# An attention and mixture layer on one Trainium2 core: the start and the end of the program are written in another order

## The reference, cut to what matters

```python
xn = _layernorm(x)
q = (einsum('bte,oe->bto', xn, Wq) + bq) * 16 ** -0.5
kv = einsum('bte,oe->bto', xn, Wkv) + bkv             # k, v: 16 channels each
qr = q.reshape(b, 16 * 512, 16)                       # 8192 query rows a batch
p = softmax(einsum('brd,bsd->brs', qr, k))
attn = heads_back(einsum('brs,bsd->brd', p, v)) @ Wo.T + bo
# mixture: e of 6 experts by xn @ w_gate (the largest), tokens = A @ B
a = softmax(xn @ tokens[e].T / 16)
delta = ((a[:, 1:] @ (tokens @ wt.T + wt_b)[1:] + xn) @ wd.T + wd_b) * scale
out = x + attn + xn + log(exp(delta) for the chosen expert)
```

## Time and profile before

| | |
|---|---|
| median of three runs | 924.08 us (920.78 to 924.17) |
| profiled execution | 922.81 us |
| its span, first to last instruction | 921.0 us |
| PE busy | 857.4 us, 93% of the span |
| DVE busy | 780.7 us, 85% |
| ACT busy | 673.2 us, 73% |
| POOL busy | 512.8 us, 56% |
| mean granted TensorE clock | 0.971 |
| chain of waits that ended last | PE 78%, DVE 15%, issue 3%, POOL 2% |

### The profile page before, as it was taken

The page is one execution under the profiler, slowest core; times in us unless marked ns, Lnnn a source line. Parts: engine busy times, 40 slices in busy tenths (PEclk is TensorE's granted clock), DMA queues, the critical chain, the costliest instruction groups (busy, mean ns, idle before and its releaser), DMA issues.

```text
span 921.0 us, 17722 instructions
## 1 busy us (share of the span) xinstructions
PE 857.4 (93%) x5845; PEld 282.1 (31%) x5845; DVE 780.7 (85%) x1490; ACT 673.2 (73%) x1369; POOL 512.8 (56%) x691
## 2 busy tenths in 40 slices
PE   4479999999999999999999999999999999999895
PEld 2223222332323333332323333332333333232222
DVE  6578898988989898998989898998989898899814
ACT  2115787787878778777877877787778778788880
POOL 2656566565666656565666647566666656534200
PEclk9676999999999999999999999999999999999998
DMA  3423243534524453543335353442444453331110
GB/s 96 97 66 60 74 92 92 117 83 116 113 75 105 107 114 94 124 87 108 95 94 111 94 116 87 129 100 86 96 113 104 104 115 84 92 94 61 48 60 34
DMA packets 125072, 86.04 MB, mean 93 GB/s; under 512 B 57143, under 2 KB 109112, under 8 KB 124984
## 3 DMA queue, kind: packets, MB, share of 16 engines
q1 hardware_dynamic: 124824, 84.82, 38.3%
q10 hardware_dynamic: 160, 0.10, 0.1%
HBM read 39.30 MB, written 33.54 MB: 79 GB/s over the span
## 4 chain that ended last, share of the span: by engine, by line
PE 78%; DVE 15%; issue 3%; POOL 2%; ACT 1%; DMA 1%; ACTq 0%; POOLq 0%; DVEq 0%
PE pO L364 24%; PE pA L346 18%; DVE M L808 9%; PE pB L351 8%; PE pA L481 5%; PE pA L428 5%; PE pA L499 4%; PE pA L483 3%; PE pA L417 3%; PE pA L453 2%; PE pA L468 2%; DVE st L728 2%; PE pB L461 1%; DVE RL L821 1%; PE pB L439 1%
## 5 line engine op out<-in xcount | busy, mean ns | idle before, releaser
L808 DVE TENSOR_REDUCE M<-pA 128x1 f32<-128x512 f32 x1024 | 652.3, 682 | 86.4 <-PE pA L346 82.3
L627 ACT ACTIVATE P<-pB 128x512 f32<-128x512 f32 x1002 | 552.6, 601 | 130.5 <-PE pB L351 126.0
L346 PE MATMUL pA<-K,Q 48*128 48x512 f16 x1024 | 326.0, 388 | 21.7 <-DVE M L808 11.8
L351 PE MATMUL pB<-Q,K 50*128 50x512 f16 x1002 | 317.8, 385 | 0.3 <-DVE M L808 0.3
L364 PE MATMUL pO<-P,VK 128*32 128x512 f32 x2048 | 273.7, 607 | 3.1 <-ACT OTr L633 2.0
L346 PEld LDWEIGHTS pA<-K,Q 48*128 48x128 f16 x1024 | 67.8, 94 | 343.6 <-DVE M L808 287.7
L954 POOL TENSOR_SCALAR Cz<-Cx 128x512 f32<-128x512 f32 x32 | 62.1, 1940 | 37.0 <-ACT Cx L609 37.0
L499 PE MATMUL pA<-wo,On 128*128 128x256 f32 x248 | 71.9, 414 | 2.7 <-DVE RL L821 2.7
L364 PEld LDWEIGHTS pO<-P,VK 128*32 128x32 f32 x2048 | 40.4, 108 | 99.3 <-issue 63.2
L351 PEld LDWEIGHTS pB<-Q,K 50*128 50x128 f16 x1002 | 64.3, 94 | 11.8 <-ACT P L627 10.3
L968 POOL TENSOR_TENSOR On<-Op,Rb 128x512 f32<-128x512 f32 x31 | 39.9, 1286 | 45.0 <-issue 41.2
(11 more groups left out here) (148 smaller groups left out, 806.6 us busy)
## 6 DMA issues: line engine op xcount, KB each, us to landing
o_parts<-OTr SPq DMA_DIRECT2D x62, 256.0 KB, 2.3
X<-in_x SPq DMA_DIRECT2D x16, 512.0 KB, 3.9
q_pieces<-Qp SPq DMA_DIRECT2D x64, 128.0 KB
out<-OUT SPq DMA_DIRECT2D x32, 256.0 KB, 3.9
Op<-o_parts SPq DMA_DIRECT2D x31, 256.0 KB
Rb<-l_parts SPq DMA_DIRECT2D x31, 256.0 KB
Q<-q_pieces SPq DMA_DIRECT2D x30, 256.0 KB, 4.8
Q<-q_pieces SPq DMA_DIRECT2D x34, 128.0 KB, 4.5
```

The source lines that it names most:

```text
L346: e.matmul(bank1("ab", t)[:, :], Q16[r:r + 48, b % 3, h, 128 * s:128 * s + 128], K16[r:r + 48, b % 3, :], start=True, stop=True).then_inc( ...
L351: e.matmul(bankB(t)[:, :], K16[r:r + 50, b % 3, 128 * i:128 * i + 128], Q16[r:r + 50, b % 3, :, 32 * hh:32 * hh + 32], start=True, stop=Tr ...
L627: e.activation(P[:, u % PR, :], bankB(u + LB)[:, :], ACT.Exp, scale=alpha).then_inc(S("e"))
L808: e.tensor_reduce(M[:, t // 32 % 2, t % 2, t % 32 // 2:t % 32 // 2 + 1], bank1("ab", t)[:, :], AX, ALU.max, negate=True).then_inc(S("mx"))
```

## The change

Batch 1 gets a table of its own, `SECOND`, and its x is loaded in the setup, ahead of the biases. Its statistics and normalisation come before batch 0's first tile. 56 and 12 products of a 128x128 identity with itself, written to `pO`, are put ahead of `rg` and behind `bs` (`warm0`, `warm1`). `uke` of batch 0 goes from VectorE to ScalarE, and `vge` of batch 0 before the K DMAs. Each of the two writes of Q to HBM waits only for its own piece. `bw0`, `bw1`, `w2` go from before the first tile to slots 6.4 to 12.4, and the first batch's `s` to `radd0` four slots later. At the end the second products of the last 44 tiles go in fours instead of twos, `o0` to `o3` of the last batch follow the last two `pv`, and `sl0` and `o3` take a bank of the second group and `sl1` one of the first.

```diff
+    "utm": -30, "s": 9, "smax": 9.6, "sexp": 10.2, "ssum": 10.8, "snorm": 11.4, "p": 17, "pte": 17.6, "a": 21, "mm": 21.6,
+SECOND = {
+    "stats0": -125.9, "stats1": -125.8, "stats2": -125.7, "stats3": -125.6, "aggr": -125.5, "var": -124, "root": -115.3,
+    "refine": -113.9, "norm": -113.8, "ph": -113.6, "pl": -107, "xtd": -102.5,
+}
...
-        put("ab", n - n % 2 + 0.02 * (n % 2), n)
+        put("ab", n - n % 2 + 0.02 * (n % 2) if n < NT else n - n % 4 + 0.02 * (n % 4), n)
...
-            "bd": lambda t: (S("e"), t - LB + 1), "sl0": lambda b: (S("rl"), 4),
+            "bd": lambda t: (S("e"), t - LB + 1), "sl1": lambda b: (S("rl"), 8),
...
-            "sl1": lambda b: (S("rl"), 8),
+            "sl0": lambda b: (S("rl"), 4),
+            "o3": lambda b: (S("fo"), 4 * b + 4),
...
+                for k, count in enumerate((56, 12)):
+                    if due(f"warm{k}", n) is not None:
+                        w.wait_ge(S("id"), 4)
+                        for _ in range(count):
+                            e.matmul(pO[:, 0:128], idh[:, :], idh[:, :], start=True, stop=True)
...
+                if due("uke", n) == 0:
+                    w.wait_ge(S("uk"), 1)
+                    w.wait_ge(S("bks"), 3)
+                    e.activation(UK[0:UKW, :], bank1("uk", 0)[0:UKW, :], ACT.Identity, scale=uks[0:UKW, 0:1],
+                                 bias=ukb[0:UKW, 0:1]).then_inc(S("uke"))
...
+            e.dma_start(X[:, 1, :, :], x[1].rearrange("(i p) c -> p i c", p=128)).then_inc(S("x_1"), 16)
             e.dma_start(bo_s[:, :], bo.partition_broadcast(128)).then_inc(S("bo"), 16)
...
-                if (b := due("load", n)):
+                if (b := due("load", n)) and b > 1:
...
-                        w.wait_ge(S(f"ql{g}"), b + 1)
                         w.wait_ge(S(f"qr_{b % 2}"), 64 * (b // 2))
                         for k in range(2):
+                            w.wait_ge(S(("qh", "ql")[k] + str(g)), b + 1)
```

More of the change, by code:

```diff
@@ L79 @@
 PARTH_LAST = {"lr": 86.2, "or": 86.3, "rec": 88.8, "lw": 89.4, "rb": 92.2, "on": 98.3}
-PE_NAMES = ("ab", "pv", "rg", "xt0", "xt1", "bs", "bw0", "bw1", "w2", "uk", "q0", "q1", "vg", "vt", "s", "p", "a", "d0", "d1",
+PE_NAMES = ("ab", "pv", "warm0", "warm1", "rg", "xt0", "xt1", "bs", "bw0", "bw1", "w2", "uk", "q0", "q1", "vg", "vt", "s", "p", "a", "d0", "d1",
             "d2", "d3", "mt", "o0", "o1", "o2", "o3", "sl0", "sl1", "oa0", "oa1", "oa2", "oa3", "ob0", "ob1", "ob2", "ob3")
-ACT_NAMES = ("root", "xh0", "xh1", "wh", "wdh", "kd", "alpha", "bwe0", "bwe1", "w2e", "qe0", "qe1", "vge", "vte", "sexp", "pte", "dexp0",
+ACT_NAMES = ("root", "xh0", "xh1", "wh", "wdh", "kd", "alpha", "bwe0", "bwe1", "w2e", "uke", "qe0", "qe1", "vge", "vte", "sexp", "pte", "dexp0",
              "dexp1", "dexp2", "dexp3", "dlog0", "dlog1", "mte", "ex", "ot")
@@ L288, in build, with turns @@
             "w2": lambda b: (S("w2e"), 1), "xt0": lambda b: (S("xl"), 1), "xt1": lambda b: (S("xl"), 2),
-            "sl1": lambda b: (S("rl"), 8),
+            "sl0": lambda b: (S("rl"), 4),
+            "o3": lambda b: (S("fo"), 4 * b + 4),
         }
-        def turns(freed, first, last):
+        def turns(freed, first, last, o3):
             return sorted((n, name, key) for name in freed for n, key in at[name].items()
-                          if name != "ab" or first <= key < last and key not in at["bd"].values())
-        TURNS = (turns(FREED1, 0, NT), turns(FREED2, LB, NT + LB))
+                          if (name != "ab" or first <= key < last and key not in at["bd"].values())
+                          and (name != "o3" or key in o3))
+        TURNS = (turns(FREED1, 0, NT, range(NB - 1)), turns(FREED2, LB, NT + LB, (NB - 1,)))
         TURN = tuple({(name, key): k for k, (_, name, key) in enumerate(t)} for t in TURNS)
@@ L303, in bank2, with bankO @@
             return R2[TURN[1][name, key] % N2]
+        def bankO(t, b):
+            return (bank2 if (t, b) == (3, NB - 1) else bank1)(f"o{t}", b)[:, 0:C]
         def bankB(t):
@@ L498, in _ @@
                         for part in range(parts):
-                            mm = e.matmul(bank1(f"o{t}", b)[:, 0:C], On[:, b % 2, part, 128 * t:128 * t + 128],
+                            mm = e.matmul(bankO(t, b), On[:, b % 2, part, 128 * t:128 * t + 128],
                                           wo[:, part, :], start=(part == 0), stop=(part == 1))
@@ L751, in _ @@
                                         xT[:, 0, :, 0, c, :], ALU.subtract).then_inc(S("xl"))
-                if (b := due("uke", n)) is not None:
+                if (b := due("uke", n)):
                     w.wait_ge(S("uk"), b + 1)
```

29 lines of the change are left out of this document (13 added, 16 removed), and 2 rows, old and new, of the table SETUP.

## The result

The changed kernel takes 901.49 us (899.26 to 902.46, four runs) against 923.74 of the kernel before: a ratio of 0.9762 [0.9734, 0.9791], 22 us off. A second set of runs on another occasion gave 900.23 against 921.32, 0.9772 [0.9754, 0.9790]. The profiled execution took 902.32 us, 0.8 above its median, with a span of 900.4; that is 20.6 less than before.

The account below looks back on a forecast made before the run. TensorE's products were taken to bound the middle (98% busy), leaving gains at both ends: 8.6 at the start plus 8.4 at the end, 17.0 off 922.8, gave 905.8, stated as 906.5 us; range 902.5 to 912.0.

Parts of the forecast that it names:

- `q0` of batch 1 at 37.8: At the start: batch 1's first projection begins at 37.8 us instead of 47.95, 10.15 sooner.
- `w2` charged with 1.5 us: Behind `q0` of batch 1: `w2` takes 2.00 us at the low clock, 0.5 covered, cost 1.5 (bounds 0 and 2.0).
- the fours counted as nothing: Last 44 tiles: ScalarE close to full, so fours count nothing (between 0 and 1.5 gained).
- Where the gain lies: Middle from 77.6 to 872 us keeps its time; the gain is 8.6 at the start and 8.4 at the end.
- The warm products: Setup on TensorE: 56 identity products at 0.15 us each end at 10.3, under the wait to 10.84, costing nothing.
- they hold the clock up, each projection takes 1.47: Batch 0's projections from 16.06 us: if identity products hold the clock up, each takes 1.47 instead of 2.72.
- clock low again at `q0`: Rival at batch 0's projections: clock falls after the 56 products, 2.2 us lost, 908.7; chance 0.25.
- better than the sum by over 3 us: Whole kernel: clock high through the first 44 tiles and fours that fill ScalarE; chance 0.05.
- the stop at the two tiles: Start, behind `s`: two tiles run from 36.6 to 37.8 us before `q0` of batch 1.
- a low clock in the last products: Rival at the end: last output products at 0.92 us each, a loss of 4, 910.8; chance 0.12.
- an overrun of the warm products: Rival in the setup: identity products at 0.257 us each, 5.5 late, 912.0; chance 0.04.
- a slow transpose: Rival at the start: mkT, xT and Q's reads delay each other, xT lands later, no gain, 915.1; chance 0.03.

Follow-up runs that it names:

- in the gap: Changed kernel plus 50 identity products behind batch 0's `vt` transpose and 12 ahead of the last transpose of maxima: 900.16 us.
- second profile: The changed kernel run and profiled once more, unaltered: 900.23 us.

## Why the prediction was wrong in its size

The mechanisms were the ones forecast. The step that failed is the sizing of three terms of the sum, all in the same direction: `q0` of batch 1 at 37.8 (36.83 measured), `w2` charged with 1.5 us (about 0.6), and the fours counted as nothing (1.3). With them the range ended too early.

*Where the gain lies.* Right: the middle keeps its 795.6 to 795.8 us, the gain is at the ends and in the mechanisms named. The stop before `q0` of batch 1 goes by the early load and normalisation, shown by taking both back (9.8 us). The end goes by the `pv` and the banks, 8.2 + 0.4 us measured against 8.1 + 0.3; taking the order back costs 3.5 of it, and how the rest divides was not run.

*The warm products.* Right that they cost nothing, wrong in price and in use. 0.15 us each was taken between 0.107 and 0.257; they take 0.105 here and 0.081 to 0.107 over the ten profiles that have them, the lower bound or less. The Trainium skill, TensorE: Matmul & The Clock Gate, Back-to-back issue gap, gives N/1.2 cold and N/2.4 + 2.5 ns warm for products taken by themselves, 107 and 56 ns at 128 columns, and about 81 ns for a stream in which each product has its weight load. Each product here has one, and the runs still lie at the first two, with 0.105 here and 0.059 in the gap (50 in 2.96 us). By "they hold the clock up, each projection takes 1.47" `q0` should have taken 1.47; it took 2.14 to 2.72 in those ten profiles: behind 2.96 us of idle time the granted clock is 0.88 from 10 to 11 us and 0.50 from 11 to 16. So the rival "clock low again at `q0`" was the true course at that place. Its price of 2.2 us was not paid: in the first profile the clock rose while `q0` ran, `uk` behind it took 1.46, and `KS` started at 20.39 (21.41 without the products, and 21.45 in the second profile with them). And without the products, where `q0` of batch 1 is late by 1.0, the first second product comes at 66.93 against 67.04. The step from "later at `q0` of batch 1" to "later at the end" failed, because the clock behind `q0` gives the microsecond back: it is high sooner there, as the 1.10 us of `w2` show. The row given for that rival, half speed behind 7.15 us of idle time, does not show that such a wait lowers the clock: in that trace the granted clock had been 0.50 since 30 us.

*Up to `q0` of batch 1.* 37.8 was forecast, 36.83 measured, though the first tile came at 27.91 and not at 27.3. The Q reads went out at 23.13 (22.9 forecast), and the tile waited for their landing. UTm started at 32.86, not 33.4, as the mask's transpose landed 2.7 us after its issue and not 3.24; the two tiles behind `s` took TensorE 0.7 us (from the end of `s` at 36.15 to 36.83), not 1.2, as VectorE had emptied the banks by then and the pace of the maxima did not bind (its last maximum ended at 34.7). With those the DMA transpose's landing became the last limit (0.15 to 0.21 us of waiting for it in six of the eight profiles with the early normalisation and the 68 products).

*`w2`.* 1.5 us were charged, about 0.6 was paid: the stretch from `q0` of batch 1 to the first second product grew from 29.65 to 30.21. The term was its time at the low clock less what VectorE had left. What it missed is, I take it, that VectorE's maxima set much of the stretch behind it (26.3 us busy of 30.2), so that TensorE catches up. The run with `w2` ahead of the first tile could not test this, as its clock ran otherwise there.

*The fours.* "I count nothing (between 0 and 1.5 gained)": 1.3 measured. ScalarE was taken as full there, but it had idle pieces, the largest of 0.98 and 0.69 us, while TensorE made a `pv` and output products at the low clock between two pairs of tiles (ScalarE's timeline of the kernel before, then of the changed kernel):

```profile
877.60 0.60 ACT L627 ACTIVATE P<-pB 128x512 f32<-128x512 f32 x1 [0.98 <-PE pA L351]
...
879.37 0.60 ACT L627 ACTIVATE P<-pB 128x512 f32<-128x512 f32 x1 [0.69 <-PE pA L351]
```

```profile
868.46 0.60 ACT L648 ACTIVATE P<-pB 128x512 f32<-128x512 f32 x1 [1.56 <-PE pA L360]
```

With fours these two pieces become one of 1.56 us, nearly as long; what goes are three small ones of 0.23 to 0.29 farther on, in whose place one of 0.20 is left. Over the stretch ScalarE's idle time falls from 2.54 to 1.76 us and its listed busy time from 23.61 to 23.07, which together is the 1.3. That twos cost 1.3 us is shown; that they do so through the number of stops of ScalarE is read from these rows.

*The sum.* 17.0 against 20.5 in the profiles: 2.0 more at the start, 1.3 for the fours, 0.2 elsewhere at the end. The rest up to 22.2 by the medians is spread of single executions: the profile before stood 0.9 under its median, the profile after 0.8 over it.

*The range.* It stopped at 902.5 because "better than the sum by over 3 us" was given 0.05. But the open terms, the fours (0 to 1.5), `w2` (0 to 1.5 charged) and the stop at the two tiles (1.2 charged), reach 4.2 us under 906.5, to 902.3, and a kernel's single runs spread by 1.5 us and more to either side. All three terms lay on the cheap side, by 1.3, 0.9 and 0.5; the prediction had taken the dear end or the middle of each, so the range should have reached to 900.

Of the other rivals, a low clock in the last products, an overrun of the warm products and a slow transpose came in no profile of the changed kernel.

## What to carry to other kernels

Look for the engine whose queue holds the next batch's preparation behind work that is needed later, and move the preparation ahead as far as its DMA allows; here this one move, with the load of x that it needs, was worth nearly the whole gain of the start. At an end, put the products that the longest remaining chain waits for ahead of those that only fill banks, and give the latter banks that nobody has to empty first. Products made only to raise TensorE's clock should be tested by taking them out: here a rise before a sparse stretch did not last, and a kernel that reached the dense stretch 1.0 us later had the high clock sooner within it.

## What the hardware showed that I had not expected

The same program has a high or a low clock in the same place in different executions: behind a wait of 1.35 us with the same work before it, a `pv` took 1.94 us in one and 1.07 in the other. The column of the granted clock reads 1.00 from 0 to 10 us while 56 products of 128 columns take 0.105 us each, which is the pace of 1.2 GHz, and in the kernel before it reads 1.00 up to 28 us while `q0` takes 2.72 us at 16.06; in these traces the column is not to be trusted ahead of its first change. And ScalarE's exponentials are listed with up to 0.98 us in the last stretch (882.29) while most start 0.48 us apart, so here their listed length is not their price.
